# GpSimd's second eight scatters of a chunk placed ahead of its three residual additions

## The reference

```python
x = _layernorm(x + _L0_attn_ref(x, ...))       # conv, minGRU, feed-forward: "the mixer"
x = _layernorm(x + _L0_xattn_ref(x, ctx, ...)) # 16 heads, causal mask over 120 context rows
x = _layernorm(x + _L0_ffn_ref(x, ...))        # MoE: shared MLP + top-2 of 16 experts

# in _L0_ffn_ref
router_logits = jax.nn.sigmoid(x @ gate_w + gate_b)
expert_values, expert_indices = jax.lax.top_k(router_logits, k=2)
expert_values = expert_values / jnp.sum(expert_values, axis=-1, keepdims=True)
selected = jnp.take_along_axis(all_outputs, expert_indices[..., None], axis=2)
return x + _mlp(x, shared_wg, shared_wu, shared_wd) + jnp.sum(expert_values[..., None] * selected, axis=2)
```

## Time and profile before

| | |
|---|---|
| median of 3 timed runs | 1636.52 us (1636.0 to 1638.09) |
| the profiled execution's own time | 1619.51 us |
| its span, first to last instruction | 1617.8 us |
| TensorE busy / weight loads | 83% / 68% |
| VectorE, ScalarE busy | 59%, 59% |
| GpSimd busy | 52% |
| mean granted TensorE clock | 0.938 of full speed |

### The profile page before, as it was taken

How to read it: one execution, slowest core, us unless ns; L and a number is a source line. 1 busy time by engine, 2 the same in 40 slices (tenths; PEclk the granted TensorE clock), 3 DMA queues, 4 the chain that set the end, 5 groups by cost and what they waited for, 6 DMA issues and landing times. The chain is left out here.

```text
span 1617.8 us, 34460 instructions
## 1 busy us (share of the span) xinstructions
PE 1348.5 (83%) x11280; PEld 1098.5 (68%) x11280; DVE 956.1 (59%) x2616; ACT 946.5 (59%) x3395; POOL 834.8 (52%) x988
## 2 busy tenths in 40 slices
PE   2889897999898988899898998989988998967542
PEld 1667676777786777678776777767776777756442
DVE  3456565565655666566764777556665776555324
ACT  3666656576756666466755667565665766555111
POOL 4343525543555457554556546654566646547244
PEclk9999998999998999889998999989999999989777
DMA  6000000032212312222212212132122212135563
GB/s 207 8 7 8 7 7 15 26 93 59 60 38 83 96 30 67 63 79 78 64 43 69 81 55 71 42 99 79 37 60 82 82 57 61 37 94 154 157 181 84
DMA packets 149425, 109.99 MB, mean 68 GB/s; under 512 B 12736, under 2 KB 144384, under 8 KB 149248
## 3 DMA queue, kind: packets, MB, share of 16 engines
q1 hardware_dynamic: 139328, 89.43, 19.0%
q0 software_dynamic: 8192, 16.79, 3.6%
q10 hardware_dynamic: 1728, 1.57, 0.3%
HBM read 73.14 MB, written 34.60 MB: 67 GB/s over the span
## 5 line engine op out<-in xcount | busy, mean ns | idle before, releaser
L1791 POOL TENSOR_TENSOR pr<-pr,ri 128x480 f32<-128x480 f32 x256 | 251.1, 995 | 303.4 <-DVE ri L1394 299.9
L1068 ACT ACTIVATE pr<-sE,nm 128x120 f32<-128x120 f32 x512 | 178.1, 360 | 240.3 <-DVE nm L1389 222.3
L1056 ACT ACTIVATE pT<-t 120x512 f32<-120x512 f32 x256 | 142.3, 614 | 78.7 <-PE t L528 72.8
L1068 ACT ACTIVATE pr<-sO,nm 128x120 f32<-128x120 f32 x512 | 179.2, 381 | 0.0
L669 PEld LDWEIGHTS sE<-kT,qT 64*128 64x128 f32 x1024 | 131.1, 197 | 55.3 <-issue 55.3
L711 PE MATMUL pvb<-wo,hT 128*128 128x128 f32 x1024 | 137.4, 290 | 31.7 <-DVE hT L1404 31.7
L669 PE MATMUL sO<-kT,qT 64*128 64x120 f32 x1024 | 156.7, 295 | 7.0 <-issue 7.0
L1404 DVE TENSOR_TENSOR hT<-pvb,col 128x512 f32<-128x512 f32 x128 | 87.9, 686 | 126.0 <-PE pvb L702 111.4
L711 PEld LDWEIGHTS pvb<-wo,hT 128*128 128x128 f32 x1024 | 125.8, 200 | 45.5 <-DVE hT L1404 45.0
L669 PE MATMUL sE<-kT,qT 64*128 64x120 f32 x1024 | 155.7, 295 | 0.5 <-issue 0.5
L1820 POOL DMA_INDIRECT sorted_x<-x,slot x128 | 129.8, 1014 | 47.3 <-issue 34.3
(11 more groups left out here) (382 smaller groups left out, 3525.7 us busy)
## 6 DMA issues: line engine op xcount, KB each, us to landing
wq<-in_w_e SPq DMA_DIRECT2D x232, 128.0 KB
sorted_y<-yq SPq DMA_DIRECT2D x68, 256.0 KB
xq<-sorted_x SPq DMA_DIRECT2D x58, 256.0 KB
xt<-in_x SPq DMA_DIRECT2D x16, 256.0 KB, 2.9
sorted_x<-yq SPq DMA_DIRECT2D x16, 256.0 KB, 4.2
cT<-in_ctxT SPq DMA_DIRECT2D x16, 240.0 KB, 3.0
out_y<-y SPq DMA_DIRECT2D x48, 64.0 KB
sorted_x<-x,slot POOLq DMA_INDIRECT x128
```

Source lines behind the costliest of these rows:

```text
L1056: f(pT[:, 4 * r:4 * r + 4, :], seqs((t0, t1)[r][0:S, :]), ACT.Copy).then_inc(sem[f"probsT{r}_sb"], 1)
L1068: ins = f(pr[:, p % RING, r, i, :], score_banks[r][:, i * S:(i + 1) * S], ACT.Exp, bias=nm[:, p % 2, r, i:i + 1], accum_out=rsum[:, p % 2, ...
L1791: GP.tensor_tensor(pr[:, p % RING, r, :, :], pr[:, p % RING, r, :, :], ri[:, p % 2, r, :, :].to_broadcast([P, 4, S]), ALU.mult).then_inc(s ...
```

## The change

The block with the eight scatters moves up in GpSimd's `body`, from behind `a_residuals(a)` to ahead of `a_x1_bo(b)`. Nothing else changes: the same instructions with the same waits, in another order on one queue.

```diff
@@ -1857,13 +1857,13 @@
                     a_ln1(b)
                 if A:
                     a_normed(a, 0)
+                if C and c and c % 2 == 0:
+                    for n in range(CHUNK, 2 * CHUNK):
+                        c_scatter(c // 2 - 1, n)
                 if B:
                     a_x1_bo(b)
                 if A:
                     a_residuals(a)
-                if C and c and c % 2 == 0:
-                    for n in range(CHUNK, 2 * CHUNK):
-                        c_scatter(c // 2 - 1, n)
                 if es:
                     gathers(es, 0, 4)
```

## The result

The changed kernel took **1614.85 us** (median of 6 runs, 1609.47 to 1624.29) against 1636.26 us (6 runs, 1627.1 to 1638.09) for the kernel before: ratio **0.9895, 95% interval [0.9868, 0.9923]** (the quotient of the two medians is 0.9869, at the interval's edge). The mechanism that I weighed at 28 in 100 (a real stall, made shorter) is the one at work, with another size than I gave it. On another chip, met in the experiments, no stall was seen, and the change in b = 5 to 13, where the gain lies, brings nothing (the whole change was not run there).

What follows compares the result with a forecast made beforehand. TensorE, busy for 83% of the span, was taken as the bound, so time moves only where it waits. Terms 0 + 0 - 2.5 - 3 - 1.3 = -6.8 us from 1636.5 gave about 1630 us, range 1606 to 1640.

Steps and rivals of the forecast that it cites:

- a real stall, made shorter: Rival: delay around the indirect-DMA burst is in timed runs and the cut ends it; 1608 us, 28 in 100.
- the rival's case: The real stall ended by the cut: 1608 us, 28 in 100; the range held most of it.
- Item 1: GpSimd's queue, step heads: additions still take their time, division still at +23.7 in b = 5; 0 us.
- GpSimd's floor: b = 5 to 13, odd: GpSimd's late queue keeps `b_probs_T` from coming before +24.7 to +25.7.
- Item 2: Step heads: x1b, xm and xz come 10.1 us later but covered; 0 us, at most 1 us a step.
- Item 3: Scatters end 3.9 us earlier, so `x_load` and expert weights do: -2.5 us in b = 3, -3 us over five steps.
- Item 4: b = 15: scatters fill GpSimd's 1.56 us wait for VectorE's x1, shortening the queue to the division; -1.3 us.
- Item 5: Odd steps: engines crawl during the twelve-DMA burst; cutting it worth up to -27 us, taken as 0 in timed runs.
- the common steps of 0.7 us: In the stall, recorded instructions start 0.7 us or multiples apart; read as records queueing, given 6 in 10.
- My own test at the end of the prediction: Profile about 25 us shorter: if the median falls as much, stall real; if by 7, it belongs to recording.
- The slower rival: Odd steps: stall real, cut doesn't drain it, block starts ahead of first row maxima; 1661 us, 8 in 100.
- the price of +36: b = 5: an undrained stall would put TensorE at `b_probs_T` at about +36 instead of +31.3.

Runs made afterwards that it cites:

- before2: The kernel before, unchanged, run once more on chip 8 for its trace: 1631.65 us.
- early12: Against the changed kernel: the four gathers follow the moved scatters at once, ahead of the additions, so the burst stays twelve; chip 1, 1625.13 us, ratio 0.9988 to before.
- only5to13: Against the kernel before: the change made only in b = 5, 7, 9, 11 and 13; chip 13, 1554.29 us, ratio 1.0003.
- after2: The changed kernel, run once more on chip 8 beside the kernel before: 1614.36 us, ratio 0.9872.
- eight: Against the kernel before: the four head gathers of b = 5 to 13 (odd) moved into the loop; chip 13, 1558.68 us, ratio 1.0034.
- spread2: Against the changed kernel: head scatters removed, all 16 in the loop as 2, 2, 1, 3, 1, 2, 3, 2; chip 13, 1548.94 us, ratio 0.9973 to before.
- eight2: Against the kernel before: the four head gathers of b = 5 to 13 (odd) moved into the loop; chip 8, 1602.91 us, ratio 0.9800.

## Why the prediction was right or wrong

**The sum was 0 + 0 - 2.5 - 3 - 1.3 = -6.8 us. Measured on chip 8: -21.4 us** (1635.73 to 1614.36). The forecast has the right sign for the wrong reason, and the result lies in the range only because the range took in the rival's case.

*Item 1, GpSimd's floor stays: right.* Division at +23.7 before, +23.6 after.

*Item 2, the additions come later at no cost: wrong.* I asked who reads x1b, xm and xz, and found them covered. I didn't ask which engine the additions hold up while they run. At +15 to +19 they meet `sg` or `tsum` on VectorE, and take 3.2 us from the chain qT, scores, maxima, `b_probs_T`. At their old place (+4.8 to +8.5) no VectorE operation that runs beside them is stretched, in any step of before2. That is some 3 us in each of six steps: the bound of 1 us a step was too small.

*Item 3, `xq` and the expert weights earlier: the wait exists, the gain does not.* On the chip without a stall `d_T` waits 2.93 us for `xq` in b = 3, against the 2.6 that I computed. But with the new order VectorE is late at the same place and, on a chip with the stall, the burst falls on the first scores, so b = 3 grew by 1.4 us (86.1 to 87.5) where I had -2.5; and early12 gives 0.9988 with `xq` just as early. Of the -3 us for the five other steps nothing is to be seen in the time: only5to13 gives 1.0003, with the earlier `xq` and the blocked `tsum` together.

*Item 4, b = 15: the queue's size right, its worth wrong.* The last gather ends at +17.4 in place of +19.0, but the division behind it wasn't held by GpSimd's queue, in before2 (first row, L1781 at 1407.05) or in after2 (second row, L1781 at 1390.01):

```profile
1430.50 1.93 POOL L1791 TENSOR_TENSOR pr<-pr,ri 128x480 f32<-128x480 f32 x2 [4.43 <-DVE ri L1394]
1412.59 1.93 POOL L1791 TENSOR_TENSOR pr<-pr,ri 128x480 f32<-128x480 f32 x2 [5.20 <-DVE ri L1394]
```

On chip 13 `b_probs_T` of b = 15 is at +20.7 with the eight scatters at the head (only5to13, eight) and without them (spread2), so the queue is worth nothing there. On chips with the stall it came at +29.0 and +30.5 in the two traces of before, and at +28.2, +28.2 and +27.0 in the three of the change: whatever is gained there is gained from the stall, not from the queue. The tail of after2 is 4.1 us shorter than that of before2, but that of my first profiles 3.5 us longer (216.1 to 219.7), so a share of b = 15 in the gain is not shown.

*Item 5, the stall at 0 in timed runs: this is the step that failed.* I reasoned from the common steps of 0.7 us that the delay sits with the records, and from that to "timed runs write no such records". Nothing that this case had shown stood behind the second half. Every timed run comes with a span of its own, 1.7 us below its time, and early12 and the change, which start the scatters and issue `xq` at the same time and differ in whether the burst is cut, are 21 us apart in timed medians, though in b = 5 to 13 the change alone carries the blocked `sg`. My own test at the end of the prediction decides it too: the profile fell by 21.1 us (before2 to after2) and the median by 21.4.

The first half may well hold: the chips with the stall lose 252 to 386 records and the chip without it 1 to 4. The Trainium skill's rule that the recording block applies back pressure (NOTIFIC — the notification-queue block, section 7.1) would go with that. But the missing records can be the cause, or a second effect of the same congestion. Whether an execution that nothing records would stall was not tried, and no run here can tell.

*The size of the stall's part.* I gave the real stall 5.6 us a step, down to GpSimd's floor. It was 3.2. The cut alone would be worth more: twelve to eight takes 5.7 us from the second maxima (27.2 to 21.5, eight2), and in the change, where VectorE is blocked for 3.2 us and the burst starts earlier, 2.5 of them are left (24.7). The slower rival's picture was seen in part: the stall begins before the first row maxima are done (+13.5 and +14.9 against +12.2 and +12.8). But it is over by the second maxima: from them to `b_probs_T` it is 3.7 us (+24.7 to +28.4), as in b = 6 (+18.3 to +22.0), in spite of the four gathers, and the price of +36 did not come.

## What to carry to other kernels

A step that is moved on GpSimd's queue must be asked two things: who waits for its result, and which VectorE operations run beside it at its new place. Keep indirect DMAs apart: with eight of twelve 2.3 us apart, chip 8 showed no delay in the head of b = 5, where a row of twelve at 1.27 us delayed TensorE, VectorE and ScalarE; and don't trust a row because it is short, since rows of three in the loop were followed by some 3 us of delay. And where a profile shows a delay that looks like the profiler's, measure whether the timed runs carry it before setting it to zero; two orders that differ only in that delay are enough.

## What the runs showed of the hardware

The same program took 1631.79 us on chip 1, 1635.73 on chip 8 and 1553.51 on chip 13 (medians): 5% between chips. Each chip was met once, so whether this belongs to the chip for good isn't shown. The kernel before has no trace on chip 13; of the 79 us between the spans of before2 (chip 8) and only5to13 (chip 13, changed in b = 5 to 13 only), 32 lie in the odd steps, 33 in the tail and 12.5 in the even steps, all of which hold rows of three indirect DMAs or more. The tail takes 214 to 223 us against 190 with before's order or the change's in it; it was not taken apart further. The first three steps, which hold no such row, agree within 3 us (245 to 248, where they hold the order of before or after), and b = 4 to 0.02 us, so a slower clock or slower engines are not what makes the difference. A change that shortens this stall was worth 1.5% and 1.3% on the first two, and its part in b = 5 to 13 nothing on the third, so its ratio means little without the chip.

A run of eight indirect DMAs at 1.27 us made the second row maxima 3.2 us late, of twelve 8.9 us; eight at 1.14 us with an eighth of the rows, and four gathers behind them, 11 to 13 us; twelve with eight of them at 2.3 us, none; four alone at the head of a step, none. But TensorE fell 2.9 us behind at a row of three (1.3 to 1.5 us apart) in the loop of b = 6. What tells that row from the harmless four was not found.

GpSimd's three additions of 128x512, back to back, stretched a VectorE operation of 0.16 us to 3.33 us: until the last of them ended.
